# Last batch of a selective scan: every fourth product with B made by GpSimd instead of VectorE

## The reference, cut to what matters

```python
def step(h, inp):
    dt_t, B_t, C_t, u_t = inp
    dA = jnp.exp(dt_t[:, :, None] * A)
    h = h * dA + (dt_t * u_t)[:, :, None] * B_t[:, None, :]
    y = jnp.einsum('bcs,bs->bc', h, C_t)
    return (h, y)
...
y = jnp.swapaxes(ys, 0, 1) + u * D_skip
y = y * silu(z)
return jnp.einsum('blc,dc->bld', y, W_out)
```

## Time and profile before

| what | value |
|---|---|
| median of 3 runs | 2736.17 us (2722.61 to 2740.17) |
| the profiled execution | 2718.45 us |
| its span, first to last instruction | 2716.7 us |
| DVE busy | 1655.2 us (61%), 2411 instructions |
| POOL busy | 961.1 us (35%), 559 instructions |
| PE busy | 2245.3 us (83%) |
| mean granted TensorE clock | 0.889 |
| scan stage, first to last scan | 1287.10 to 2267.64 us of the span |
| last batch, first to last scan | 2034.84 to 2267.64 us of the span |

### The profile page before, as it was taken

One profiled execution on the slowest core, in us unless ns is written; L12 is line 12 of the kernel. 1 busy time (PEld: TensorE's weight loads), 2 busy tenths in 40 slices (PEclk: granted clock), 3 DMA queues, 4 the chain that ended last, 5 costly groups with the idle time before them and its releaser, 6 DMA issues. The chain is left out here.

```text
span 2716.7 us, 26080 instructions
## 1 busy us (share of the span) xinstructions
PE 2245.3 (83%) x7794; PEld 1114.4 (41%) x7794; DVE 1655.2 (61%) x2411; ACT 1225.8 (45%) x1655; POOL 961.1 (35%) x559
## 2 busy tenths in 40 slices
PE   3989699978997799947788798879987667998994
PEld 1425542454345533633233243334324224665662
DVE  4454345523562355043999999999999994112774
ACT  1682258314851376216365445545554332443442
POOL 0000000000000000003888888876777663211563
PEclk9689777987699759969999999999999999998997
DMA  3000100010000100071988897889888995222444
GB/s 107 1 1 1 63 16 1 1 50 29 1 1 16 47 1 1 0 96 52 307 255 258 285 298 258 265 268 306 280 281 284 328 317 185 86 84 70 123 139 145
DMA packets 156645, 360.26 MB, mean 133 GB/s; under 512 B 46151, under 2 KB 74698, under 8 KB 155419
## 3 DMA queue, kind: packets, MB, share of 16 engines
q1 hardware_dynamic: 144474, 327.70, 37.8%
q0 software_dynamic: 12032, 30.82, 3.9%
HBM read 325.51 MB, written 37.12 MB: 133 GB/s over the span
## 5 line engine op out<-in xcount | busy, mean ns | idle before, releaser
L941 POOL TENSOR_TENSOR late<-late,rows 128x1024 f32<-128x1024 f32 x256 | 610.6, 2388 | 206.9 <-DVE late L1383 194.9
L1383 DVE TENSOR_TENSOR_SCAN late<-m_Q,late 128x1024 f32<-128x1024 f32 x256 | 586.2, 2290 | 40.4 <-ACT m_Q L1107 11.6
L1524 PE MATMUL m_Q<-late,ident_m 128*128 128x512 f32 x1024 | 504.8, 621 | 107.0 <-POOL late L941 107.0
L1107 ACT ACTIVATE m_Q<-late,acol 128x1024 f32<-128x1024 f32 x256 | 286.1, 1118 | 465.7 <-DVE late L1383 463.3
L227 POOL TENSOR_TENSOR aT<-kr 128x1024 f32<-128x1024 f32 x8 | 15.1, 1892 | 1070.3 <-ACT kr L435 1070.3
L1524 PEld LDWEIGHTS m_Q<-late,ident_m 128*128 128x128 f32 x1024 | 192.3, 198 | 398.7 <-issue 209.7
L1376 DVE TENSOR_TENSOR late<-m_Q,rows 128x1024 f32<-128x1024 f32 x256 | 307.3, 1200 | 4.7 <-DMA rows<-bc_s 3.2
L335 DVE SCALAR_TENSOR_TENSOR rr<-turns,work 128x1024 f32<-128x1024 f32 x128 | 156.2, 1220 | 173.8 <-ACT turns L418 173.8
L418 ACT ACTIVATE turns<-work,rnd 128x1024 f32<-128x1024 f32 x128 | 142.1, 1110 | 127.0 <-PE work L517 85.7
L1261 ACT ACTIVATE late<-m_Q,e_b1c 128x128 f32<-128x128 f32 x312 | 88.9, 367 | 205.4 <-PE m_Q L1590 205.4
L1602 PE MATMUL m_Q<-rows,late 128*128 x624 | 156.8, 395 | 6.0 <-ACT late L1261 4.7
(11 more groups left out here) (225 smaller groups left out, 3448.0 us busy)
## 6 DMA issues: line engine op xcount, KB each, us to landing
rows<-bc_s SPq DMA_DIRECT2D x512, 512.0 KB, 5.5
r_s<-late SPq DMA_DIRECT2D x39, 256.0 KB, 2.0
xin<-in_x SPq DMA_DIRECT2D x4, 1024.0 KB, 5.7
xres<-in_x SPq DMA_DIRECT2D x4, 1024.0 KB, 8.4
mx_s<-s SPq DMA_DIRECT2D x4, 1024.0 KB, 4.5
xn_s<-xh SPq DMA_DIRECT2D x4, 1024.0 KB, 4.4
xn1T_s<-kr SPq DMA_DIRECT2D x4, 1024.0 KB, 4.8
early<-xn1T_s SPq DMA_DIRECT2D x4, 1024.0 KB, 7.3
```

What stands on the lines that cost most here:

```text
L941: nc.gpsimd.tensor_tensor(pr[:, n % NH, :], h[:, n % NH, :], cb[:, n % NCB, :], ALU.mult).then_inc(pr_ok, 1)
L1107: A(dA[:, :], dt[:, (b * KI + m) % 2, :], ACT.Exp, scale=acol[:, m, i % NS:i % NS + 1]).then_inc(dA_ok, 1)
L1383: v_.tensor_tensor_scan(h[:, n % NH, :], dA[:, :], dB[:, n % 2, :], 0.0, ALU.mult, ALU.add).then_inc(h_ok, 1)
L1524: ins = mm(half(Y, c), ident[:, :], half(pr[:, n % NH, :], c), start=False, stop=(n % NS == NS - 1), skip_group_check=True)
```

## The change

In the last batch, the B product of every fourth step (the fourth, eighth, ... of its 64: 16 in all) is taken off DVE and made by POOL. At a step i of the batch with i % 4 == 0, POOL does times_c(i) and then the product of step i+3, before what `besides` puts there and before times_c(i+1). It can't read `du` in PSUM, so it makes its own dt * u once a tile into an SBUF buffer (`dus`, in buffer 1 of `u`), at the tile's first step; the product goes to `dBp`, in buffer 1 of `zs`. For the first tile it must wait for tile 11 to be done with these buffers: for its skip matmuls and for its gate (`yg_ok`). The waits of SP, of `drive` and of `scan` on a product go to one of two semaphores.

```diff
+        def shared(n):
+            return n >= LAST and n % 4 == 3
...
-                        sp.wait_ge(dB_ok, n - NBB + 1)
+                        wait_product(sp, n - NBB)
...
+                def drive_shared(t):
+                    pool.wait_ge(dt_ok, t + 1)
+                    if t == (B - 1) * KI:
+                        pool.wait_ge(y_full, t * NS)
+                        pool.wait_ge(yg_ok, t)
+                    else:
+                        pool.wait_ge(dBp_ok, shared_below(t * NS))
+                    nc.gpsimd.tensor_tensor(dus[:, :], dt[:, t % 2, :], u[:, t % NU, :], ALU.mult).then_inc(dus_ok, 1)
+
+                def times_b(n):
+                    pool.wait_ge(b_in[n % NBB], 16 * (n // NBB) + 16)
+                    pool.wait_ge(dus_ok, n // NS - (B - 1) * KI + 1)
+                    if n > LAST + 3:
+                        pool.wait_ge(h_ok, n - 3)
+                    nc.gpsimd.tensor_tensor(dBp[:, :], dus[:, :], bb[:, n % NBB, :], ALU.mult).then_inc(dBp_ok, 1)
...
+                        if b == B - 1 and i % NS == 0:
+                            drive_shared(b * KI + i // NS)
+                            times_b(b * STEPS + i + 3)
+                        elif b == B - 1 and i % 4 == 0:
+                            times_b(b * STEPS + i + 3)
...
-                        dv.wait_ge(dB_ok, t * NS)
+                        wait_product(dv, t * NS - 1)
+                        wait_product(dv, t * NS - 2)
...
-                    dv.wait_ge(dB_ok, n + 1)
+                    wait_product(dv, n)
...
-                        times_b(n + 1)
+                        if not shared(n + 1):
+                            times_b(n + 1)
```

More of the change, by code:

```diff
@@ L795, in phase_me @@
         sig_ok = sem("m_sig_ok"); silu_ok = sem("m_silu_ok"); soft_ok = sem("m_soft_ok"); dt_ok = sem("m_dt_ok"); du_ok = sem("m_du_ok")
[L796 removed]
+        dA_ok = sem("m_dA_ok"); dB_ok = sem("m_dB_ok"); dus_ok = sem("m_dus_ok"); dBp_ok = sem("m_dB_gpsimd_ok")
         h_ok = sem("m_h_ok"); pr_ok = sem("m_pr_ok"); y_full = sem("m_y_full"); yg_ok = sem("m_yg_ok")
@@ L809, in tile_at, with shared_below, wait_product @@
             return b * NQT + TILES.index((kind, m))
+        LAST = (B - 1) * STEPS
+        dus = u[:, ((B - 1) * KI - 1) % NU, :]
+        dBp = zs[:, ((B - 1) * KI - 1) % NU, :]
+        def shared(n):
+            return n >= LAST and n % 4 == 3
+        def shared_below(n):
+            return max(0, (n - LAST) // 4)
+        def wait_product(e, n):
+            if shared(n):
+                e.wait_ge(dBp_ok, shared_below(n) + 1)
+            else:
+                e.wait_ge(dB_ok, n + 1 - shared_below(n))
         half = lambda ap, c: ap[:, c * CH:(c + 1) * CH]
@@ L1379, in scan @@
                     dv.wait_ge(dA_ok, n + 1)
-                    dv.wait_ge(dB_ok, n + 1)
+                    wait_product(dv, n)
                     if n >= NH:
                         dv.wait_ge(pr_ok, n - NH + 1)
-                    v_.tensor_tensor_scan(h[:, n % NH, :], dA[:, :], dB[:, n % 2, :], 0.0, ALU.mult, ALU.add).then_inc(h_ok, 1)
+                    drive_term = dBp[:, :] if shared(n) else dB[:, n % 2, :]
+                    v_.tensor_tensor_scan(h[:, n % NH, :], dA[:, :], drive_term, 0.0, ALU.mult, ALU.add).then_inc(h_ok, 1)
                 def gate(t):
```

## The result

The changed kernel takes 2748.69 us in the median of 20 runs (2725.16 to 2762.99), the kernel before 2737.8 in 20 (2703.79 to 2752.07). The ratio is 1.0058, with a 95% interval of 1.0030 to 1.0085: slower by 8 to 23 us. The forecast was 2743 us and +7.

A forecast was written before the change was run, and what follows sets the result against it. The decay on ACT, held by the single dA buffer, was taken to set the 3.54 us step, not DVE. Terms 0 + 1.6 + 1.1 + 4.5 = +7 us on 2736 gave 2743 us, range 2729 to 2765; likeliest case +4 to +11, chance 0.60.

The forecast's parts named there:

- The removed products are worth 0: DVE's 16 removed products, 19.2 us busy, lie in gaps where the decay ends last: 0 on the path.
- The added work, 20 x 2.35 = 47 us: POOL's 16 products and 4 drives in the last batch, at 2.35 us each.
- The gate's wait, +1.6 at step 3: POOL's first drive waits for the gate of tile 11, so scan 3 starts late: +1.6 us.
- The row's wait, +1.1 at scan 7: POOL's product 7 waits for its B row, 5.6 us in landing, and delays scan 7: +1.1 us.
- Skip and identity matmuls on PE keep their order and have idle time: 0: The matmuls on PE were to add no time to the last batch: 0.
- 5.6 + 2.4 = 8.0 fits: In later rounds, row landing plus product fit the 10.6 us after scan i starts; no scan waits, by small margins.
- The drives, +4.5: DVE's drives of tiles 13, 14, 15 meet a busy POOL and wait: +2.1, +1.2, +1.2 us.
- Changes under 1% can't be told from none: Whole-kernel times: changes under 1% (27 us) aren't told from none, as three runs lie 18 us apart.
- the first (only the first wait remains): Drives find POOL in a gap and step 7's row lands in time: +1.6 to +3, 2739 us; chance 0.18.
- The second (starved drives): The three drives each wait out several GpSimd operations, 4.78 to 7.02 us: +14 to +20 in all, 2753 us; chance 0.14.
- The third (GpSimd the bound): GpSimd sets the pace between shared products, slower by over 1%: some +31, 2767 us; chance 0.06.
- The fourth: The product was on the path, or nothing else becomes late: 2717 us at the most, 0.7% faster; chance 0.02.

The follow-up runs named there:

- Experiment 1: Changed kernel with the 16 products made nowhere, neither on VectorE nor on GpSimd; last batch 238.51 us, 0.9966 of the time before.
- experiment 8: Kernel before, with a second buffer for dA from step 44 of the last batch; all products on VectorE; last batch 236.69 us.
- experiment 9: Kernel before with a second dA buffer from step 44, and products of steps 51, 55, 59 and 63 made by GpSimd; last batch 239.18 us.
- the repeat: The changed kernel profiled once more, unaltered, to see how far its last batch repeats; last batch 246.86 us.
- experiment 3: Changed kernel, but step 3 stays on VectorE and GpSimd's first drive comes at step 4, 15 products shared; last batch 249.98 us.
- experiment 5: Changed kernel, with ScalarE's copies of TensorE's half-tiles and the softplus one step later in the last batch; last batch 246.78 us.
- experiment 6: Changed kernel, but GpSimd's product takes the C row just used in place of the B row still to land; last batch 244.97 us.
- Experiment 4: Changed kernel, but the product of each tile's last step stays on VectorE, 12 shared; last batch 242.05 us.
- experiment 11: Kernel before, with only the indirect DMAs behind each tile's last C product moved behind the next C product; 0.998 of the time before.
- experiment 7: Changed kernel, step 3 kept on VectorE, GpSimd making the product of step i+2 ahead of C product i; last batch 245.54 us.
- experiment 2: Changed kernel with GpSimd's added work kept, but VectorE makes all its products too and the scans use those; last batch 249.54 us.

## Why the prediction was right, and where it wasn't

The time (2743 forecast, 2748.69 measured), its direction and the likeliest case were right; the stage's cost was 10.1 us where the sum said 7, at the upper end of the +4 to +11 given for that case. That it came so near is partly luck: a term of +1.1 didn't come, and one of +3.45 that the sum had at 0 did. By its steps:

- **The removed products are worth 0: right, and shown.** Experiment 1 removes them for free and gains nothing; the idle time before 15 shared scans ends on the decay. The reason given, the single dA buffer, is shown by experiments 8 and 9: with two buffers a removed product gave 1.3 us at step 51.
- **The added work, 20 x 2.35 = 47 us: right.** GpSimd's busy time in the last batch rose from 162.92 to 208.24 us, by 45.3.
- **The gate's wait, +1.6 at step 3: right** (1.64, also in the repeat). Yet without it experiment 3 was 2.5 us slower, not faster, a part of that beside TensorE's low clock.
- **The row's wait, +1.1 at scan 7: wrong in place.** GpSimd did wait for the row, 0.91 us, but scan 7 had by then been put off by the stalls of scans 5 and 6, and started on time after scan 6. With these stalls gone (experiment 5) it shows, 0.65.
- **"Skip and identity matmuls on PE keep their order and have idle time: 0": the step that failed.** Their order is the point: the half-tiles for ScalarE stand behind the identity matmuls, which wait for late C products, and the decay stands behind ScalarE's copies. That is 0.38 + 1.09 + 0.56 + 0.58 + 0.84 = 3.45 us, and experiment 5, in which all five are gone, shows the path. At step 41 TensorE's clock has a part: after an idle wait of 4.99 us four identity matmuls took 3.47 us instead of 1.98, at a granted clock of 0.60 (2186 to 2190). The 10.6 us that I gave GpSimd for the product also missed this: its C products had less slack than its B products.
- **"5.6 + 2.4 = 8.0 fits" for later rows: right for the scans, short for GpSimd.** No later scan waited for a shared product with the change, but GpSimd stood 21.9 us at rows with C products queued behind, and experiment 6 shows that these waits are what made it late at the first drive.
- **The drives, +4.5: right in mechanism and sum** (4.95). Singly 2.1, 1.2, 1.2 were forecast and 1.23, 1.84, 1.88 measured; the third was 0.09 in the repeat, and the sum 3.3. So the mechanism is right, and the near match of the sum is luck within the scatter of a single drive. Experiment 4 removes them by letting GpSimd catch up in time.
- **Changes under 1% can't be told from none: wrong.** With 20 runs of each kernel the interval is 0.30 to 0.85% slower, and zero lies outside it.

Of the rivals, the first (only the first wait remains) is out. The second (starved drives) didn't come: 3.08 us was the longest. What I had put against it, that the long drives need GpSimd's DMAs, got no support from the only DMA that I moved alone (experiment 11). The third (GpSimd the bound) is out: after step 3 no scan waited for a shared product, and from step 48 to 63 the time is 53.95 us in both kernels. The fourth is out by experiment 1.

The rule cited ahead, from the Trainium skill's page "SBUF — State Buffer", section "SBUF: two separate sides" (whoever starts first keeps the pair of ports for its whole instruction), agrees with the drives of 2.44 to 3.08 us and not with the 7.00 us of experiment 11, in which the drive came 1.1 us after a C product's start and was let in only after two more operations.

What stays open: why a drive waits for one GpSimd operation in the last two batches and for two or three in the first two. In both, GpSimd's operations stand back to back and the drive comes inside one of them. Also open is whether any of the measured +0.58% (8 to 23 us) beyond the last batch's 10 us is the change; what follows the last gate varied by 23 us between two profiles of the changed kernel.

## What to carry to other kernels

An engine that is 97% busy in a stage may still not set its pace. Look at what ends the wait of the step that matters, and ask which other work of the same length lies beside the work you want to take away; here a single buffer between ScalarE and VectorE kept 1.2 us of product a step off the path. Work put on an engine with slack makes a debt of lateness with everything queued behind it: follow it through each engine that works in order (here C product, TensorE, ScalarE's copy, decay) and not only to its own consumer. Where one stall of such a debt was mended, others grew (experiments 3 and 5); only less work (experiment 4, 242.05 us), or less waiting for transfers (6 and 7, 244.97 and 245.54), took a part of it away.

## What the runs showed of the hardware that I had not expected

- TensorE's own clock can be a part of the debt. Its granted clock was 0.50 (1.2 GHz) beside the stalls of experiments 2 and 3, and a pair of half-tile matmuls took 2.07 us there instead of 1.12; the late start of scan 6 in experiment 2 was 2.71 us instead of 1.09. In experiment 3 TensorE had been idle for 5.27 us before it, waiting for a C product. In experiment 2 the waits before it were 2.21 and 1.58 us, and with the change nearly the same waits (1.98 and 1.60) were followed by a clock of 1.00: what decides isn't shown. The same happens without late C products: 0.79, 1.15 and 1.16 us at step 5 in experiments 1, 7 and 9, after clocks of 0.50, 0.66 and 0.61 (over 4 to 8 us) that followed TensorE's wait for the gate. The kernel before has that low clock too (0.54 from 2042.8 to 2046.4, after 5.21 us idle), and no stall from it.
- A two-input SBUF operation of VectorE waited up to 5.8 us for GpSimd's operations back to back, in six of 16 drives of the kernel before. Moving GpSimd's DMAs by one step took that away, in a run that was 0.8% faster as a whole.
